# Relative attention: end terms stored in one piece, attention kept with features on partitions until the output stage

## The reference, cut to what matters

```python
q, k, v = proj(Wq, bq), proj(Wk, bk), proj(Wv, bv)      # (B, H, S, HD) of layernorm(x)
idx = clip(pos[None, :] - pos[:, None], -20, 20) + 20
attn = softmax((einsum('bhqd,bhkd->bhqk', q, k) + einsum('bhqd,qkd->bhqk', q, rel_k[idx])) / sqrt(HD))
o = einsum('bhqk,bhkd->bhqd', attn, v) + einsum('bhqk,qkd->bhqd', attn, rel_v[idx])
x = x + o @ Wo.T + bo
n = layernorm(x)
x = x + (silu(n @ wg.T) * (n @ wu.T)) @ wd.T
```

## Time and profile before

| | |
|---|---|
| median of 3 runs (lowest, highest) | 1385.82 us (1384.87, 1387.82) |
| the profiled execution | 1384.85 us |
| its span, first to last instruction | 1383.1 us |
| mean granted clock of TensorE | 0.972 |
| busy: PE, DVE, ACT, POOL | 1264.9, 955.0, 757.8, 551.3 us |
| project stage | to about 166 us |
| attend stage | about 167 to 1215 us |
| output stage | 1216 us to the end |

### The profile page before, as it was taken

One profiled execution on the slowest core, in us unless ns is written; L12 is line 12 of the kernel. 1 busy time (PEld: TensorE's weight loads), 2 busy tenths in 40 slices (PEclk: granted clock), 3 DMA queues, 4 the chain that ended last, 5 costly groups with the idle time before them and its releaser, 6 DMA issues. The chain is left out here.

```text
span 1383.1 us, 67607 instructions
## 1 busy us (share of the span) xinstructions
PE 1264.9 (91%) x30680; PEld 937.8 (68%) x30688; DVE 955.0 (69%) x1844; ACT 757.8 (55%) x1413; POOL 551.3 (40%) x983
## 2 busy tenths in 40 slices
PE   4387669999999999999999999999999999979998
PEld 3254437777777777777777777777777777756766
DVE  6499876776766767677767676676777776146664
ACT  4367525565655656555656566565666565623332
POOL 4376623443435343434344343534344443122221
PEclk9789959999999999999999999999999999989999
DMA  4544520111020112011111101111211110113231
GB/s 126 141 168 167 179 60 7 42 33 55 23 55 23 52 32 57 21 54 42 33 49 29 55 20 54 30 47 32 56 35 41 45 32 9 41 41 92 69 92 46
DMA packets 101541, 79.08 MB, mean 57 GB/s; under 512 B 13256, under 2 KB 97032, under 8 KB 101256
## 3 DMA queue, kind: packets, MB, share of 16 engines
q1 hardware_dynamic: 101256, 74.77, 18.3%
HBM read 45.90 MB, written 27.26 MB: 53 GB/s over the span
## 5 line engine op out<-in xcount | busy, mean ns | idle before, releaser
L1043 DVE TENSOR_REDUCE b_mx<-b_a 128x1 f32<-128x512 f32 x1024 | 658.7, 685 | 234.0 <-PE b_a L810 228.7
L1004 ACT ACTIVATE b_p<-b_s 128x512 f32<-128x512 f32 x1024 | 569.8, 595 | 399.3 <-PE b_s L851 313.6
L901 PE MATMUL b_pv<-b_p,vg 128*16 128x128 f32 x8192 | 286.7, 275 | 0.1
L774 POOL TENSOR_TENSOR qd<-q,one 48x512 bf16<-48x512 bf16 x256 | 266.2, 1040 | 28.7 <-POOLq L286 3.8
L751 POOL TENSOR_TENSOR b_np<-vg,one 128x16 bf16<-128x16 f32 x192 | 39.1, 264 | 560.7 <-DVE b_mx L1043 550.4
L851 PE MATMUL b_s<-qd,z 112*128 112x32 bf16 (+1 forms) x6016 | 248.8, 189 | 0.7 <-issue 0.6
L810 PE MATMUL b_a<-k,q 48*128 48x512 bf16 x1024 | 202.8, 393 | 26.8 <-DVE b_mx L1043 11.3
L851 PEld LDWEIGHTS b_s<-qd,z 112*128 112x128 bf16 x6016 | 205.8, 99 | 11.0 <-issue 1.0
L901 PEld LDWEIGHTS b_pv<-b_p,vg 128*16 128x16 f32 x8192 | 196.2, 96 | 21.4 <-issue 0.6
L836 PE MATMUL b_s<-q,k 54*128 54x64 bf16 (+3 forms) x4608 | 188.2, 201 | 6.4 <-issue 2.5
L836 PEld LDWEIGHTS b_s<-q,k 54*128 54x128 bf16 (+1 forms) x4608 | 126.4, 95 | 92.4 <-PE b_s L836 29.2
(11 more groups left out here) (125 smaller groups left out, 1321.8 us busy)
## 6 DMA issues: line engine op xcount, KB each, us to landing
x<-in_x SPq DMA_DIRECT2D x32, 256.0 KB, 3.2
scratch_qop<-a_parts SPq DMA_DIRECT2D x16, 384.0 KB, 2.5
scratch_kop<-a_parts SPq DMA_DIRECT2D x16, 384.0 KB, 3.2
k<-scratch_kop SPq DMA_DIRECT2D x32, 192.0 KB
q<-scratch_qop SPq DMA_DIRECT2D x32, 192.0 KB
scratch_v<-a_vr SPq DMA_DIRECT2D x16, 256.0 KB, 3.2
k<-scratch_kop SPq DMA_DIRECT2D x32, 128.0 KB
q<-scratch_qop SPq DMA_DIRECT2D x32, 128.0 KB
```

The lines of the kernel that those rows point to most:

```text
L774: nc.gpsimd.tensor_tensor(dst, src, one, ALU.mult).then_inc(s["qd_ready"], 1)
L901: nc.tensor.matmul(PV[32 * a:32 * a + V16, g * P:(g + 1) * P], v[:, 0 if t <= i else 1, t, h, :], PR[at.c % 2][:, t, h, :], start=(t == 0 ...
L1004: nc.scalar.activation(out, src, ACT.Exp, scale=SCALE).then_inc(s["p_ready"], 1)
L1043: nc.vector.tensor_reduce(MX[v.c % 2][:, h:h + 1], PA[(n + hp) % NBANK][:, :], AX_X, ALU.max, negate=True).then_inc(s["a_used"], 1)
```

## The change

- Project: the end term is written once, as floats, and no longer split there (`GD` has 128 columns in place of 256; VectorE's four splitting instructions and one wide copy become one copy). PE waits for `devac` where it waited for `dsplit`, and VectorE waits for the step before's `vdone`. The matmuls of `ends` and the value projection stand as they were: the diff has no further columns of the value projection.
- Attend: GpSimd splits the end term once a batch (`end_parts`, four operations of 128x64, into `DB`) ahead of `guard_parts`. The transposes of `XT`, the division and its reciprocal go. `XT` has two buffers, and SyncE stores it with four DMAs a unit of nine partitions each (8 features and the sum) into `xo`, now (16, 9, 16, 512), after the guard rows. ScalarE's copy waits for the store of two units before. PE waits for `mt_copied` and `w_masked` where it waited for `norm`.
- Output: `xa` is loaded with features on partitions, the sums as `xd`, repeated over 8 features. VectorE takes the reciprocal of 128x512, GpSimd multiplies (`divided`), and the product is the weight operand of the output projection; attention transposes and ScalarE's copy of them go. `wo` has its rows in the new order.

```diff
-VGW = VW + 4 * T * H
+VGW = VW + 2 * T * H
...
-                        pe.wait_ge(s["dsplit"], at.count())
+                        pe.wait_ge(s["devac"], at.count())
...
-                link(nc.vector.tensor_copy(db[:, 0, :], pd[:, :]))
-                nc.vector.tensor_tensor(dr[:, :], pd[:, :], db[:, 0, :], ALU.subtract).then_inc(s["dsplit"], 1)
+                nc.vector.tensor_copy(GD[p][:, T * H:], pd[:, :]).then_inc(s["devac"], 1)
+                if at.since(1):
+                    dve.wait_ge(s["vdone"], at.count())
                 maxima(0)
-                dve.wait_ge(s["dsplit"], at.count(1, 1))
-                link(nc.vector.tensor_copy(db[:, 1, :], dr[:, :]))
-                link(nc.vector.tensor_tensor(db[:, 2, :], dr[:, :], db[:, 1, :], ALU.subtract))
-                nc.vector.tensor_copy(GD[p][:, T * H:], db[:, :, :].rearrange("p c n -> p (c n)"))
                 maxima(1)
...
-    XT = m.sb("b_xt", [P, NQ4 * P])
-    XN = [m.sb(f"b_xn{p}", [P, E]) for p in range(2)]
-    RD = m.sb("b_rd", [P, H])
...
+            def rows_out(at):
+
+                sp.wait_ge(s["xt_ready"], at.count(1, 1))
+                rows = d["xo"][at.it * 2 + at.c // T][:, :, at.c % T * P:(at.c % T + 1) * P]
+                for a in range(NQ4):
+                    sp.dma_start(rows[:, NQ4 * a:NQ4 * (a + 1), :],
+                                 XT[at.c % 2][32 * a:32 * a + HD + 1, :].rearrange("p (g q) -> p g q", g=NQ4)).then_inc(xo_out[at.c % 2], 16)
...
                 if at.plus(1).exists():
                     guard_rows(at.plus(1))
+                if at.since(1):
+                    rows_out(at.plus(-1))
...
-                if at.since(2):
-                    sp.wait_ge(s["norm"], at.count(1, -1))
-                    sp.dma_start(d["xo"][bass.ds(at.count(1, -2), 1)].rearrange("o p c -> (o p) c"), XN[at.c % 2][:, :])\
-                        .then_inc(xo_out[at.c % 2], 16)
+                        sp.wait_ge(xo_out[p], NXO * T)
 
             run_all(unit, PER, U)
             for p in range(2):
                 load_rows(sp, k, d, p, p)
-            for u in (U - 2, U - 1):
-                sp.wait_ge(s["norm"], u + 1)
-                sp.dma_start(d["xo"][u], XN[u % 2][:, :]).then_inc(xo_out[u % 2], 16)
+            rows_out(at0(U - 1))
...
+            def end_parts(at):
+
+                p = (at.c // T) % 2
+                batch = at.it * 2 + at.c // T
+                pd = VG[p][:, VW + T * H:VW + 2 * T * H]
+                one = k["one"][:, 0:1].to_broadcast([P, T * H])
+                pool.wait_ge(v_in[p], (at.even(T) + 1) * 32)
+                nc.gpsimd.tensor_tensor(DB[p][:, 0, :], pd, one, ALU.mult).then_inc(s["ends"], 1)
+                pool.wait_ge(s["ends"], batch * NEND + 1)
+                nc.gpsimd.tensor_tensor(DR[:, :], pd, DB[p][:, 0, :], ALU.subtract)
+                nc.gpsimd.tensor_tensor(DB[p][:, 1, :], pd, DB[p][:, 0, :], ALU.subtract).then_inc(s["ends"], 1)
+                pool.wait_ge(s["ends"], batch * NEND + 2)
+                nc.gpsimd.tensor_tensor(DB[p][:, 2, :], DR[:, :], DB[p][:, 1, :], ALU.subtract).then_inc(s["ends"], 1)
...
+                if i == 0:
+                    end_parts(at)
...
-                    e = VW + (T + c * T + i) * H
-                    nc.gpsimd.tensor_tensor(np_[:, 3 + c], heads(VG[p][:, e:e + H]), one, ALU.mult)
+                    nc.gpsimd.tensor_tensor(np_[:, 3 + c], heads(DB[p][:, c, i * H:(i + 1) * H]), one, ALU.mult)
...
-            def output_transposes(at):
-                pe.wait_ge(s["xt_ready"], at.count(1, 1))
-                for g in range(NQ4):
-                    ins = nc.tensor.transpose(MI[:, g * P:(g + 1) * P], XT[:, g * P:(g + 1) * P], k["ident"][:, :])
-                ins.then_inc(s["xtt_ready"], 1)
...
-                                pe.wait_ge(s["norm"], at.count(1, -1))
-                            else:
-                                pe.wait_ge(s["mt_copied"], 2)
+                                pe.wait_ge(s["w_masked"], at.count(1, -1))
+                            pe.wait_ge(s["mt_copied"], at.count(1, 1))
...
-                    if c == 3 and before.exists():
-                        if at.plus(1).exists():
-                            pe.wait_ge(s["mt_copied"], at.count(1, 2))
-                        output_transposes(before)
...
-                if at.since(1):
-                    act.wait_ge(s["xtt_ready"], at.count(1))
-                nc.scalar.copy(XT[:, :], PV[:, :]).then_inc(s["xt_ready"], 1)
+                if at.since(2):
+                    act.wait_ge(xo_out[at.c % 2], at.even(1) * NXO)
+                nc.scalar.copy(XT[at.c % 2][:, :], PV[:, :]).then_inc(s["xt_ready"], 1)
...
-            def normalise(at):
-                dve.wait_ge(s["xtt_ready"], at.count(1, 1))
-                v = MI[:, :].rearrange("p (n c) -> p n c", c=32)
-                nc.vector.reciprocal(RD[:, :], v[:, :, HD]).then_inc(s["rd"], 1)
-                dve.wait_ge(s["rd"], at.count(1, 1))
-                if at.since(2):
-                    dve.wait_ge(xo_out[at.c % 2], at.even(1) * 16)
-                xn = XN[at.c % 2][:, :].rearrange("p (a g d) -> p g a d", a=NQ4, d=HD)
-                nc.vector.tensor_tensor(xn, MI[:, :].rearrange("p (g a c) -> p g a c", g=NQ4, a=NQ4)[:, :, :, 0:HD],
-                                        bc(RD[:, :].rearrange("p (g a) -> p g a", g=NQ4), 3, HD), ALU.mult).then_inc(s["norm"], 1)
...
-    sp.dma_start(k["xa"][p][:, :, :], d["xo"][bass.ds(batch * T, T)].rearrange("t p e -> p t e")).then_inc(k["rows_in"][p], 16)
+    sp.dma_start(k["xd"][p][:, :], bc(d["xo"][batch][HD], 0, HD)).then_inc(k["rows_in"][p], 16)
+    sp.dma_start(k["xa"][p][:, :], d["xo"][batch][0:HD].rearrange("d h s -> (d h) s")).then_inc(k["rows_in"][p], 16)
...
+            def divided(at):
+                x = XA[at.c % 2]
+                pool.wait_ge(x_in[at.c % 2], at.even(1) * NIN + NIN)
+                pool.wait_ge(s["inv"], at.count(1, 1))
+                nc.gpsimd.tensor_tensor(x[:, :], x[:, :], XD[at.c % 2][:, :], ALU.mult).then_inc(s["divided"], 1)
+
...
                 if at.plus(2).exists():
+                    divided(at.plus(2))
                     biased(at.plus(2))
...
-                pe.wait_ge(s["aTs"], at.count(1, 1))
+                pe.wait_ge(s["divided"], at.count(1, 1))
                 if at.since(1):
                     pe.wait_ge(s["x1"], at.count())
                 for t in range(T):
-                    ins = nc.tensor.matmul(py[:, t * P:(t + 1) * P], aT[:, t * P:(t + 1) * P], k["wo"][:, :], start=True, stop=True)
+                    ins = nc.tensor.matmul(py[:, t * P:(t + 1) * P], XA[at.c % 2][:, t * P:(t + 1) * P], k["wo"][:, :], start=True, stop=True)
                 ins.then_inc(s["y"], 1)
...
-                if at.plus(2).exists():
-                    attention_transposes(at.plus(2))
...
+            def inverse(at):
+                x = XD[at.c % 2]
+                dve.wait_ge(x_in[at.c % 2], at.even(1) * NIN + NIN)
+                nc.vector.reciprocal(x[:, :], x[:, :]).then_inc(s["inv"], 1)
...
                 hidden(at, 2)
+                if at.plus(2).exists():
+                    inverse(at.plus(2))
                 dve.wait_ge(s["down"], at.count(1, 1))
...
+                            ("v", (B, P, S), F32), ("guard", (B, P, VGW - VW), F32), ("xo", (B, HD + 1, H, S), F32)):
...
-        "wq": by_d(a["attn_Wq"]).T, "wk": by_d(a["attn_Wk"]).T, "wv": a["attn_Wv"].T, "wo": a["attn_Wo"].T,
+        "wq": by_d(a["attn_Wq"]).T, "wk": by_d(a["attn_Wk"]).T, "wv": a["attn_Wv"].T, "wo": by_d(a["attn_Wo"].T),
```

More of the change, by code:

```diff
@@ L537, in constants @@
                         nc.vector.memset(k["vg"][p][:, 0:VW].rearrange("p (n c) -> p n c", c=V16)[:, :, HD:HD + 1], 1.0)
-            def linker(at, done):
-                def link(ins):
-                    nonlocal done
-                    done += 1
-                    ins.then_inc(s["dv"], 1)
-                    dve.wait_ge(s["dv"], at.count(NLINK, done))
-                return link
             def statistics(at):
@@ L609, in stage_attend @@
     MT = m.sb("b_mt", [6 * H, P], BF16)
+    DB = [m.sb(f"b_db{p}", [P, 3, T * H], BF16) for p in range(2)]
+    DR = m.sb("b_dr", [P, T * H])
     idb = m.sb("b_idb", [P, P], BF16)
@@ L614, in stage_attend @@
     MI = m.ps("b_mi", [P, S])
-    names = ("init", "a_ready", "a_used", "half", "s_ready", "p_ready", "w_ready", "w_masked", "pv_ready", "xt_ready", "rd",
-             "mp_ready", "mt_ready", "mt_copied", "xtt_ready", "norm", "m_in",
-             "qd_ready", "v_ready", "guard")
+    names = ("init", "a_ready", "a_used", "half", "s_ready", "p_ready", "w_ready", "w_masked", "pv_ready", "xt_ready",
+             "mp_ready", "mt_ready", "mt_copied", "m_in",
+             "qd_ready", "v_ready", "guard", "ends")
     s = {n: m.sem("b_s_" + n) for n in names}
@@ L742, in guard_parts @@
                 if i == 0:
-                    pool.wait_ge(v_in[p], (at.even(T) + 1) * 32)
```

(24 more changed lines are left out.)

33 lines of the change are left out of this document (15 added, 18 removed).

## The result

The kernel before took 1386.28 us in the runs made beside the changed one, the changed kernel 1427.84 us: ratio 1.0274, 95% interval 1.0204 to 1.0344. It is slower; the forecast was 1358.5. (The median holds one disturbed execution of 2606.79 us, which the ratio leaves out; the others took 1417.19, 1423.23 and 1432.45.) The profiled execution of the changed kernel took 1417.19 us, its span is 1415.5 (1383.1 before).

What follows compares the result with a forecast made beforehand. VectorE was taken to bound the project stage, PE attend and output. Terms -12 - 14 + 0.6 - 2 = -27.4 took the span from 1383.1 to 1355.7, the time to 1358.5 us; range 1349 to 1382.

Steps and rivals of the forecast that it cites:

- Project stage, -12: Project stage: without VectorE's four splitting instructions batches follow a 6.56 us loop, saving 12 us, from 5 to 17.
- Attend, -14: Attend: PE loses four transposes a unit, a gain of 0.92 us a batch, 14 us in all, bounds 0 to 36.
- block 1: Attend, second query block of a batch: PE could go at 727.04 in place of 727.46, gaining 0.42 us.
- Block 2: Attend, third query block of a batch: the next row pair needs no exponential, so PE gains 0.50 us.
- Rival (d): Attend: SyncE's stores make the last operand load late, PE idles up to 0.9 us in 14 batches, 1371; chance 0.08.
- Output stage, -2: Output stage: period 9.3 against 9.64 us saves 4.9, the end 0.4, the start costs 3.2; sum -2 us.
- one of four readings: Output stage, VectorE's 128x512 reciprocal: 0.78, 3.1, 4.4 or 6.1 us; 3.1 was taken.
- VectorE's loop of 9.3: Output stage: VectorE's work of 6.2 us a batch plus a reciprocal of 3.1 gives 9.3, against a period of 9.64.
- the sign: Output stage: the residual or final sum waiting for the reciprocal by over 1 us would show the forecast wrong.
- Between the stages, +0.6: Attend to output stage: four store issues replace copy, transposes, division and one store; -0.4 to +1.5, taken as +0.6 us.
- (e): Attend: ScalarE covers the removed transposes in all four query blocks, so attend gains nothing, 1372.5; chance 0.04.
- (c): Output stage: a reciprocal with small fixed part is the bound; at 6.1 us the stage costs +46, 1406; chance 0.08.

Runs made afterwards that it cites:

- the project part alone: Kernel before with only VectorE's end-term splitting taken out of the project stage and GpSimd's put into attend: 1368.58 us against 1387.03, ratio 0.987.
- the eight runs: Profiled runs of the changed kernel and seven follow-up variants that leave its attend stage alone; attend took 994.8 to 1004.1 us.
- the fillers: Changed kernel with two unread 128x512 matmuls on PE ahead of each output projection: 1403.23 us, ratio 1.0122.
- the uncoupled run: Changed kernel, every instruction kept, product written to an unread tile and projection reading the undivided rows: 1401.66 us, ratio 1.0113.
- the half reciprocal: Changed kernel with the reciprocal over 256 of the 512 columns: 1378.91 us, ratio 0.9943.

## Why the prediction was wrong

**Project stage, -12: right way, low.** Measured -19.5 and -20.6. The loop that I read as 6.56 us is 6.43 where nothing disturbs it (ScalarE's a_xnT at 117.97, 124.39, 130.82 and 137.25). Ten batches gained 14.6 (from one a_xnT to the tenth after it 82.57 us, now 67.92), not 12.3: I gave 4.3 back for the low clock, but PE, which no longer waits for VectorE, has its clock at 0.99 where it had 0.91. Against that, a step of the stretch takes 6.79 in the mean and not 6.43: 3.6 us are lost. VectorE waits there for x 11.6 us in 9 times, with the maxima queued behind that wait; that it is the cause was not tried. The other 5 to 6 are the batches outside the stretch, which I had at 3 at the most, less 0 to 4 for x.

**Attend, -14: too high.** Measured -3.6 against before, -6.5 against the project part alone. By blocks, as the prediction went through them: 0 and 3 gave nothing, as said. In block 1, PE goes on 0.64 us behind the weights at 704.32 where it was 1.08 (726.38 to 727.46), a gain of 0.44; I had 0.42. Block 2 is the step that failed:

```profile
718.33 0.12 PEld L816 LDWEIGHTS b_a<-k,q 48*128 48x128 bf16 x2 [0.46 <-issue]
718.36 0.39 PE L816 MATMUL b_a<-k,q 48*128 48x512 bf16 x2 [0.39 <-DVE b_mx L1037]
```

From the weights ahead of the transposes to the row pair it is 0.77 us (717.56 to 718.33) and it was 0.83 (740.06 to 740.89): 0.06 in place of 0.50. I wrote that a row pair "needs no exponential", and did not ask what else frees its bank: VectorE's row maximum of the pair before it. The run with short row maxima shows that. Block 1 alone makes 0.44 x 16 = 7. Against the kernel before, the changed one shows 3.6 of them, and the mean of the eight runs with its attend stage (998.9 against 999.2) 0.3. The steps from one mark to the next show where the rest went. Into block 1, 15.38 us became 14.93 where nothing disturbs it, 7.7 in all 16 batches: the gain is there in full. Into block 2 it is 15.91 and 15.88, into block 3 18.12 and 18.09. Into block 0, where the steps vary (13.6 to 14.6 in both), 1.9 are lost in all, and the last step of the stage went from 13.27 to 15.66:

```profile
1186.46 0.47 PE L922 MATMUL b_mi<-b_p,tvd 128*32 128x64 f32 x18 [2.26 <-issue]
```

PE stands 2.26 us in the middle of the last unit's products and waits for nothing that the profile shows, while the six first loads of the output stage are under way (SyncE issues them from 1175.38, some 12 us ahead of the last mark; in the kernel before four loads were issued some 24 us ahead). The same stop, 1.6 to 3.0 us, stands at the same instruction in nine of the ten kernels with the new stores and loads, and neither in the kernel before nor in the project part alone. Its cause is not shown. Several of the eight runs also show one or two short falls of the clock in attend, and the one profile of before shows none. GpSimd's four operations (0.29 to 0.31 us each) and SyncE's four stores (median 0.32 each) cost nothing behind attend's start: no wait of PE for a load or a store in the changed kernel's list from 210 to 1185. Rival (d) is out.

**Output stage, -2: wrong by 58.** The reciprocal was 3.34 us, and I had taken 3.1, one of four readings; the estimate from the Trainium skill ("VectorE: DVE Perf Modes", Walkthrough: the 8-slice pipeline in each mode), 8.3 ns a column and 4.4 us, does not hold: three sizes here, 543 ns for 64 columns, 1746 for 256 and 3343 for 512, lie on a line of 6.2 to 6.3 ns a column with some 140 to 150 fixed. VectorE's loop of 9.3 was right too (10.51 less the wait of 1.17 for loads). The start was 6.9 us from the first reciprocal to the residual (1192.39 to 1199.33), forecast 6.5. The step that failed is one sentence: "GpSimd's product lies 8 us ahead of its projection: hidden." The reciprocal for batch n+2 stands at the end of step n in VectorE's queue, and the projection of n+2 at the very start of step n+1 in PE's, directly behind the transposes that end step n. The distance between them is what PE's down matmuls and transposes take behind the third hidden product, some 2.4 us, and reciprocal and product want 4.8. I had taken the loads' lead of a batch for the product's. So I added VectorE's work and compared it with PE's, as if they only shared a period, while they formed one loop: 7.0 us from projection to the end of the third hidden product, then 3.35 + 1.46. That is 11.8, and with the low clock 13.5. The prediction had named the sign: the final sum waits over 1 us for the reciprocal (it starts at 1297.88, and PE's down matmuls had ended at 1296.6). The second failure is in what the prediction said of the clock: it priced low stretches that were there and none that a new wait might make. That is 1.7 us a batch, some 21 in all (15 periods of 195.1 us against 173.9 with the fillers).

**A hidden product would not have given 1358.5 either.** Two more terms stood at nothing. The bias addition is queued behind the product in GpSimd, and the residual needs it: in the uncoupled run, where PE does not wait for the product at all, the time is 1401.66. And "they land before the reciprocal by about 1 us" is not so: with the bias moved ahead the loads are late by about 1 us, and the time is 1379.47.

**Between the stages, +0.6:** measured 5.3 with the start of the output stage, forecast 3.8. From attend's last mark to the first residual it is 12.1 where it was 7.9, a loss of 4.3. The other 1.0 lies between the first residual and the first final sum (17.8 against 16.8), which stands behind the reciprocal of batch 2 in VectorE's queue.

**The rivals.** (e) is near the sum of attend and has the wrong mechanism: ScalarE does not cover block 1, and what covers block 2 is VectorE. (c) had the right sign and not far from the right size of the stage (+46, measured +56), by the wrong mechanism: it needs a reciprocal of 4.8 us or more. Had it been favoured, that would have been luck. No rival was a chain from the reciprocal through GpSimd to PE, and of the chance of slower, 0.09, (c) had 0.08.

**The sum.** The forecast span was 1355.7, the measured one 1415.5, 59.8 more, and the terms above make it up. The other 9.5 us of the miss lie between the profiled execution and the median, which the forecast put 1.0 above it.

## What to carry to other kernels

When a step is put at the end of one engine's round and its result is wanted at the start of another's, don't sum the engines' work: write down the loop from the consumer back to the producer with both queues' order, and compare the slack with the latency of everything in between. Invert or reduce a small array before it is copied over partitions, and in a stage whose engine has room: the same division took 54 us of VectorE as 128x512 a batch and 9 as 128x64. Price a new wait of PE twice, once as time and once as what it does to the clock of the matmuls behind it.

## What the runs showed of the hardware

A wait of 2.4 us in each 13.5 took the granted clock to a mean of 0.87, and the same wait filled with matmuls of no use left it at 1.00 and the kernel some 20 us faster (ratio 1.0122 in place of 1.0274). A wait of 0.8 us in each 10.2 (the half reciprocal) left it at 1.0. Between these it came out either way: in the uncoupled run waits of 1.75 to 2.0 us in each 11.4 left the clock at 1.00 in most batches and at 0.87 in the one named above, and of the changed kernel's waits of 2.39 one left it at 1.00.

A reciprocal of 128 partitions in f32 took 249 ns for 16 columns, 543 for 64, 1746 for 256 and 3343 for 512: about 6.25 ns a column and some 145 fixed.
